# A gated linear attention and mixture-of-experts kernel: every engine's list of operations in a new order

## The reference

```python
h = _ln(x, ln_w, ln_b)
q, k, v = h @ Wq, h @ Wk, h @ Wv
gk = log_sigmoid(h @ gk_w1 @ gk_w2 + gk_b2) / 16
S[t] = exp(gk[t]) * S[t-1] + k[t] * v[t]        # scan over the 256 tokens
o = _rms(q * S, rms_w) * silu(h @ Wg)
x1 = x + o @ Wo
x = _layernorm(x + x1 + gelu(_ln(x1) @ W1 + b1) @ W2 + b2)
scores = softmax(x @ gate_w + gate_b); top 2 of 8
for i in range(8):                               # where expert i is among the two
    out = relu((x * w_i) @ w1[i] + b1[i]) @ w2[i] + b2[i]
x = _layernorm(x + out)
```

## Time and profile before

| what | value |
|---|---|
| median of three runs | 450.14 us (448.68 to 451.42) |
| profiled execution | 452.75 us, of which 451.0 us from the first to the last instruction (the span) |
| mean granted clock of TensorE | 0.965 |
| instructions | 10568 |

### The profile page before, as it was taken

One profiled execution on the slowest core, in us unless ns is written; L12 is line 12 of the kernel. 1 busy time (PEld: TensorE's weight loads), 2 busy tenths in 40 slices (PEclk: granted clock), 3 DMA queues, 4 the chain that ended last, 5 costly groups with the idle time before them and its releaser, 6 DMA issues.

```text
span 451.0 us, 10568 instructions
## 1 busy us (share of the span) xinstructions
PE 405.0 (90%) x2806; PEld 316.7 (70%) x2806; DVE 369.5 (82%) x1216; ACT 344.5 (76%) x980; POOL 326.8 (72%) x299
## 2 busy tenths in 40 slices
PE   5998999899889888999969999788999999999993
PEld 3554555555555555477849768678899999999993
DVE  6379999999999998647875888888777877778874
ACT  2576999999888995998786689467876777777772
POOL 2057799999999997585065556777777887777775
PEclk9999999999999998899996999689999999999997
DMA  7065675765766444070001116356686877776710
GB/s 221 9 164 140 153 175 124 182 155 131 173 141 150 118 121 113 2 233 2 0 25 45 40 41 240 107 149 179 195 261 199 241 204 197 201 208 194 205 59 21
DMA packets 44378, 62.20 MB, mean 138 GB/s; under 512 B 6670, under 2 KB 29713, under 8 KB 42400
## 3 DMA queue, kind: packets, MB, share of 16 engines
q1 hardware_dynamic: 39712, 52.20, 44.9%
q0 software_dynamic: 4320, 8.93, 5.3%
q10 hardware_dynamic: 288, 0.41, 0.3%
HBM read 47.99 MB, written 13.97 MB: 137 GB/s over the span
## 4 chain that ended last, share of the span: by engine, by line
POOL 33%; PE 33%; issue 16%; DVE 10%; ACT 5%; DMA 2%; POOLq 1%; ACTq 0%; DVEq 0%
POOL states L2168 17%; PE bank L761 11%; PE bank L745 10%; POOL o_scale L2180 4%; POOL x_sb L2186 3%; PE bank L395 3%; POOL out_rows L942 3%; POOL row_buffers L2159 3%; POOL slab L2174 2%; PE bank L408 1%; ACT row_buffers L461 1%; PE bank L751 1%; PE bank L384 1%; DVE st L485 1%; PE bank L1129 1%
## 5 line engine op out<-in xcount | busy, mean ns | idle before, releaser
L596 POOL DMA_INDIRECT expert_regions<-row_buffers,row_i x64 | 62.1, 971 | 50.1 <-DVE row_i L580 22.6
L942 POOL DMA_INDIRECT out_rows<-h2t x71 | 70.7, 995 | 30.4 <-issue 24.3
L761 PE MATMUL bank<-ew,h2t 128*128 x568 | 79.1, 283 | 4.6 <-DVE h2t L893 3.2
L2168 POOL TENSOR_TENSOR states<-states,queries 128x1024 f32<-128x1024 f32 x32 | 75.1, 2370 | 7.2 <-DVE states L1906 7.2
L745 PE MATMUL bank<-h2t,slab 128*128 128x128 f32 x568 | 78.4, 282 | 0.5 <-ACT h2t L779 0.5
L761 PEld LDWEIGHTS bank<-ew,h2t 128*128 128x128 f32 x568 | 69.5, 193 | 7.6 <-issue 6.0
L1906 DVE TENSOR_TENSOR_SCAN states<-bank,kv 128x512 f32<-128x512 f32 x64 | 72.9, 1200 | 0.6 <-ACT bank L1443 0.6
L745 PEld LDWEIGHTS bank<-h2t,slab 128*128 128x128 f32 x568 | 70.7, 196 | 1.3 <-issue 0.8
L786 ACT ACTIVATE h2t<-bank,slab 128x128 f32<-128x128 f32 x142 | 43.9, 364 | 9.9 <-PE bank L745 9.9
L884 DVE TENSOR_SCALAR h2t<-bank,slab 128x128 f32<-128x128 f32 x142 | 42.6, 341 | 1.1 <-PE bank L745 0.7
L779 ACT ACTIVATE h2t<-bank 128x128 f32<-128x128 f32 x71 | 19.6, 277 | 26.8 <-PE bank L751 25.2
(11 more groups left out here) (216 smaller groups left out, 925.1 us busy)
## 6 DMA issues: line engine op xcount, KB each, us to landing
slab<-in_slabs SPq DMA_DIRECT2D x71, 258.0 KB
kv<-values_by_head SPq DMA_DIRECT2D x30, 512.0 KB, 6.0
h2t<-expert_regions SPq DMA_DIRECT2D x71, 72.0 KB
x_sb<-in_x SPq DMA_DIRECT2D x32, 128.0 KB, 6.0
values_by_head<-row_buffers SPq DMA_DIRECT2D x15, 256.0 KB, 2.1
out_rows<-h2t POOLq DMA_INDIRECT x71
expert_regions<-row_buffers,row_i POOLq DMA_INDIRECT x64
expert_regions<-pad_record SPq DMA_DIRECT2D x9, 72.0 KB, 3.0
```

The lines of the kernel that those rows point to most:

```text
L596: pool.indirect_dma_start(out=regions, out_offset=bass.IndirectOffsetOnAxis(ap=row_i[:, q, g:g + 1].bitcast(U32), axis=0), in_=rec[:, ring ...
L761: ins = pe.matmul(bank[7][:, 0:D], c_ht[:, s, c * P:(c + 1) * P], ew2[:, bass.ds(e * HC + c * D, D)], start=(c == 0), stop=(c == HC - 1 an ...
L942: pool.indirect_dma_start(out=out, out_offset=bass.IndirectOffsetOnAxis(ap=rc[:, q, D + 1:D + 2].bitcast(U32), axis=0), in_=c_y[:, item % ...
L2168: pool.tensor_tensor(half, half, queries[:, s, :].unsqueeze(1).to_broadcast([P, VL, T]), ALU.mult).then_inc(q_applied, 1)
```

## The change

The four lists of PE, ACT, DVE and POOL are new from the end of the setup to the last slot. The helper functions, their waits, the buffers and SP's list are the same, and each operation is issued as often as before. The loops over pairs and slots are written out, so that pairs and slots can differ in order. The diff has over a thousand lines of calls; these are its parts around the steps spoken of below.

```diff
@@ PE
+            transpose_x(0)
             bias_products()
-            transpose_x(0)
+            project_v(0)
             transpose_x(1)
-            project_v(0)
             project_zq(0)
+            project_v(1)
             project_g(0)
             project_k(0)
             replicate_v(0)
-            project_v(1)
             replicate_v(1)
             replicate_v(2)
             replicate_v(3)
+            transpose_x(2)
+            project_zq(1)
+            project_v(2)
             project_g(1)
             project_k(1)
...
             sum_keys(0, 0)
             sum_keys(0, 1)
-            transpose_x(3)
+            fold_ffn()
             sum_squares(0)
...
-            for k in range(5, PAIRS):
-                sum_keys(k - 3, 0)
-                transpose_second(k - 5)
-                project_k(k - 1)
-                sum_keys(k - 3, 1)
-                transpose_x(k)
-                sum_squares(k - 3)
-                project_v(k)
-                project_zq(k)
-                project_g(k)
-                output_product(k - 3)
...
             sum_squares(13)
+            output_product(12)
             first_product(0)
+            first_product(1)
             output_product(13)
-            first_product(1)
+            first_product(2)
...
+            transpose_rows(0)
             output_product(15)
-            transpose_rows(0)
             second_product(3)
             transpose_rows(1)
             logits(0)
-            first_product(5)
-            second_product(4)
             transpose_rows(2)
             logits(1)
+            second_product(4)
+            first_product(5)
+            logits(2)
...
-            for k in range(27, STEPS_C):
-                expert_step(k)
+            hidden(24)
+            back(23)
+            turn(25)
+            back(24)
+            turn(26)
+            hidden(25)
+            hidden(26)
+            turn(27)
+            back(25)
+            hidden(27)
+            turn(28)
+            back(26)
...
@@ ACT
+            squares(13)
+            sig_exp_of(15)
+            gate_sum(15)
+            sig_log_of(15)
+            z_log_of(15)
+            rstd_heads(13)
+            act.preload_act_table_set("gelu_and_others")
             evacuate_q(15)
-            norm_second(11)
-            z_log_of(15)
-            evacuate_h2t(11)
-            sig_of(14)
-            squares(13)
-            rstd_heads(13)
-            gate_sum(15)
-            act.preload_act_table_set("gelu_and_others")
             gelu(0)
             act.preload_act_table_set("natural_log_exp_and_others")
             decay_of(15)
...
             gelu(3)
+            gelu(4)
+            evacuate(0)
             act.preload_act_table_set("natural_log_exp_and_others")
+            evacuate(1)
+            rstd(0)
             rstd_second(14)
-            evacuate(0)
+            evacuate(2)
             norm_second(14)
+            exps(0)
             act.preload_act_table_set("gelu_and_others")
-            gelu(4)
             gelu(5)
...
@@ DVE
+            copy_projections()
+            stats_first(2)
+            var_first(2)
             scale_rest()
-            stats_first(2)
-            copy_projections()
+            stats_first(3)
+            var_first(3)
             first_keys()
-            var_first(2)
-            stats_first(3)
             outer_piece(0)
+            log_sigmoid(0)
             outer_piece(1)
             outer_piece(2)
-            log_sigmoid(0)
             outer_piece(3)
             scan(0)
-            copy_ffn()
-            var_first(3)
             log_sigmoid(1)
-            stats_first(4)
             outer_product(1)
             scan(1)
+            copy_ffn()
+            stats_first(4)
...
             log_sigmoid(15)
             norm_heads(13)
+            var_second(12)
+            scan(15)
             residual(13)
-            scan(15)
             stats_second(13)
             var_second(13)
             rows_of(0)
+            stats_of(0)
             norm_heads(14)
             rows_of(1)
-            stats_of(0)
+            stats_of(1)
+            split_bias()
+            norm_heads(15)
             residual(14)
...
             choice_of(0, 3)
+            places_of(0)
             logits_of(1)
-            places_of(0)
+            var_second(15)
             choice_of(1, 0)
...
@@ POOL
             norm_first(0)
             norm_first(1)
+            norm_first(2)
+            norm_first(3)
             gate_of(0)
-            norm_first(2)
             apply_q(0, 0)
             apply_q(0, 1)
-            norm_first(3)
             gate_of(1)
+            apply_q(1, 0)
             scale_of_heads(0)
...
+            apply_q(7, 0)
+            apply_q(7, 1)
+            gate_of(8)
+            sum_x(5)
+            scale_of_heads(7)
...
             apply_q(13, 0)
+            scale_of_heads(12)
             apply_q(13, 1)
+            gate_of(14)
+            sum_x(10)
+            apply_q(14, 0)
+            scale_of_heads(13)
             sum_x(11)
-            gate_of(14)
-            scale_of_heads(13)
-            apply_q(14, 0)
             apply_q(14, 1)
+            sum_x(12)
             apply_q(15, 0)
             apply_q(15, 1)
...
             scale_of_heads(15)
-            sum_x(13)
+            scatter(0, 0, 1)
             sum_x(14)
-            scatter(0, 0, 1)
             scatter(0, 1, 2)
             sum_x(15)
...
-            for item in range(21, SLOTS):
-                if BIAS_FROM <= item + 3 < SLOTS:
-                    bias_rows_in(item + 3)
-                store(item)
+            bias_rows_in(30)
+            store(21)
+            store(22)
+            store(23)
+            bias_rows_in(31)
+            store(24)
```

More of the change, by code:

```diff
@@ L1365, in _ @@
+            back(69)
+            back(70)
         @block.scalar
@@ new lines, in _ @@
+            norm_heads(0)
+            scan(2)
+            stats_first(5)
+            residual(0)
+            log_sigmoid(3)
+            var_first(5)
+            stats_second(0)
+            stats_first(6)
+            var_second(0)
+            var_first(6)
+            norm_heads(1)
+            outer_product(3)
+            residual(1)
+            scan(3)
+            stats_second(1)
+            log_sigmoid(4)
+            var_second(1)
+            outer_product(4)
+            norm_heads(2)
@@ new lines, in _ @@
+            scan(4)
+            residual(2)
+            stats_first(7)
+            stats_second(2)
+            log_sigmoid(5)
+            var_second(2)
+            outer_product(5)
+            norm_heads(3)
+            var_first(7)
+            scan(5)
+            residual(3)
+            stats_first(8)
+            stats_second(3)
+            log_sigmoid(6)
+            var_second(3)
+            var_first(8)
+            outer_product(6)
+            norm_heads(4)
+            stats_first(9)
@@ new lines, in _ @@
+            scan(6)
+            residual(4)
+            var_first(9)
+            stats_second(4)
+            log_sigmoid(7)
+            var_second(4)
+            norm_heads(5)
+            outer_product(7)
+            residual(5)
+            stats_first(10)
+            stats_second(5)
+            var_first(10)
+            var_second(5)
+            scan(7)
+            log_sigmoid(8)
+            outer_product(8)
+            norm_heads(6)
+            stats_first(11)
+            scan(8)
@@ new lines, in _ @@
+            residual(6)
+            log_sigmoid(9)
+            stats_second(6)
+            var_first(11)
+            var_second(6)
+            outer_product(9)
+            norm_heads(7)
+            stats_first(12)
+            scan(9)
+            var_first(12)
+            residual(7)
+            log_sigmoid(10)
+            stats_second(7)
+            stats_first(13)
+            var_second(7)
+            norm_heads(8)
+            outer_product(10)
+            var_first(13)
+            residual(8)
@@ new lines, in _ @@
+            scan(10)
+            stats_second(8)
+            log_sigmoid(11)
+            var_second(8)
+            outer_product(11)
+            stats_first(14)
+            norm_heads(9)
+            var_first(14)
+            scan(11)
+            residual(9)
+            log_sigmoid(12)
+            stats_second(9)
+            outer_product(12)
+            var_second(9)
+            norm_heads(10)
+            scan(12)
+            stats_first(15)
+            residual(10)
+            var_first(15)
@@ new lines, in _ @@
+            norm_first(5)
+            gate_of(3)
+            sum_x(0)
+            norm_first(6)
+            apply_q(3, 0)
+            scale_of_heads(2)
+            apply_q(3, 1)
+            gate_of(4)
+            sum_x(1)
+            apply_q(4, 0)
+            scale_of_heads(3)
+            gate_of(5)
+            apply_q(4, 1)
+            norm_first(7)
+            sum_x(2)
+            apply_q(5, 0)
```

(22 more changed lines are left out.)

1377 lines of the change are left out of this document (1097 added, 280 removed).

## The result

| | before | after |
|---|---|---|
| median of 20 runs | 451.19 us (448.19 to 452.92) | 448.00 us (445.42 to 451.39) |
| profiled execution | 452.75 us, span 451.0 | 451.34 us, span 449.5 |

The ratio is 0.9941, 95% interval 0.9922 to 0.9960: faster by 0.6%, some 3 us. The forecast was 436 us, a gain of 14. The sign was right; most of the gain that was forecast isn't there. The 20 executions of after lie up to 6 us apart, the longer ones at a lower mean granted clock (0.970 in the profiled one of 451.34 us, 0.982 to 0.986 in the five shortest), so its trace is that of one of the longest.

A forecast was written before the change was run, and what follows sets the result against it. The prediction took POOL and DVE as saturated in attention's steady part and PE in the experts', no engine bounding the whole. -8.8 - 2.0 - 4.3 + 1.0 = -14.1 gave 436 us by the median; range 429 to 448.

The forecast's parts named there:

- (a): Attention up to the end of `scan(15)`: earlier start, postponed sums and new order of the end gain 8.8 us.
- (b): From `scan(15)` to the first `transpose_rows`: 15.4 us instead of 17.4, with `split_bias` waiting for the experts' loads; gain 2.0.
- (c): Routing up to `turn(0)`: three POOL waits go, against sums among the scatters and a later first scatter; gain 4.3 us.
- (d): Experts: early slots and last scatter keep their slack, steady part nearly the old order; cost 1.0 us.
- two places where `back` follows `back`: Experts' steady part, slots 23/24 and 39/40: each exposes a relu or a row of `z_added`; +1.0 us, bounds 0 and 3.
- the gapless walk: Attention walked: `apply_q(4,0)` at 65.8 us, then POOL without gaps until `apply_q(13,1)` ends at 165.3.
- the 1.5 us for a slow first product: Attention's end: 1.5 us taken off the gain in case `first_product(0)` again runs at the lower clock; bounds 0 and 1.8.
- 2.7 from `sum_x`: Attention's end: ten sums done instead of eleven when `apply_q(13,1)` ends, bringing that point 2.7 us forward.
- the pair's handover: Rival, attention's pairs: POOL waits once per pair for a scan or `o_rs`; 458 us at 2 us a pair; chance 0.08.
- The stall by POOL's sums: Routing: two `sum_x`, four instructions, meet DVE's `choice_of(1)`; 2.0 us added, bounds 0 and 5.1.
- The lead is spent in routing: Rival: attention ends earlier, but routing keeps its pace, with no gain behind `scan(15)`; 442 to 448 us; chance 0.25.
- The change does not do what it says: Rival: start's gaps return as waits inside the pairs, routing stalls move elsewhere; 448 to 452 us; chance 0.07.

The follow-up runs named there:

- Experiment 4: The kernel after the change with only POOL's stores 0 to 10 put back among the scatters as before the change: 445.08 us, ratio 0.9890 to before.
- experiment 9: After with before's stores and the sums of pairs 14 and 15 ahead of the first scatter, plus `sum_x(10)` back ahead of `apply_q(13, 0)`: 442.48 us, ratio 0.9851.
- experiments 7 and 8: After's order to the experts, then before's: 7 moved five POOL operations later, 448.06 us; 8, also with two sums first, moved four ScalarE suppliers earlier, 444.81 us.

## Why the prediction was wrong

The sum in the trace against the forecast's terms, as lengths between the same events:

| term | forecast | trace |
|---|---|---|
| (a) to the end of `scan(15)` (191.18 to 186.38) | -8.8 | -4.8 |
| (b) from there to `transpose_rows(0)` (17.4 to 16.4 us) | -2.0 | -1.0 |
| (c) from there to `turn(0)` (80.0 to 76.25 us) | -4.3 | -3.8 |
| (d) from there to the end of the span (162.4 to 170.5 us) | +1.0 | +8.0 |
| sum | -14.1 | -1.5 |

**(d) failed as a mechanism,** and in the traces it is over half of the miss (7.0 of 12.6 us). The step was: "The last scatter moves with the first, so the records of slot 24 keep their slack." The first scatter did move, the last did not (338.19 us, 337.78 before), since stores that depend on the slots had been put ahead of scatters that don't. I had compared the order of PE's slots, not the order of stores and scatters in POOL's queue. Experiment 4 shows it: with the stores back, the last scatter moves 6.0 us and the time falls by 2 to 3 us. The term also put TensorE's clock in the first slots at nothing. From `turn(0)` to `turn(70)` after's trace takes 158.7 us, that of experiment 4 150.9 and before 151.1; of the 7.7 us between the first two, 4.0 are there at `turn(23)` and are the clock's. So 2 to 3 us of time are shown for the stores; how much the clock costs after in an execution nearer to the median, no trace shows. The other piece of the term, two places where `back` follows `back` for +1.0, had the wrong sign: from `turn(25)` to `turn(70)` after takes 88.2 us, before 89.9.

**(a) was mis-sized,** by 4.0 us, in the gapless walk. `apply_q(4,0)` comes at 67.72 instead of 65.8 (1.9), since DVE's first keys wait for PE to 19.68 instead of 17.3 (18.90 to 20.25 in the other traces with this order). From there to the end of `apply_q(13,1)` at 171.38 it is 103.7 us, not 99.5: POOL's six waits, 3.6 us, where the term allowed 1.0. The attention's end went as walked (15.0 us to the end of the scan, 14.5 in the walk), and the 1.5 us for a slow first product weren't needed: its clock stayed at 1.00. The "2.7 from `sum_x`" is worth 1.8 to 2.6 by experiment 9. Why the ring leaves POOL these waits is open: experiments 7 and 8 tried to remove them from two sides and lengthened the attention by 3.2 and 5.5 us. That is the mechanism of the rival "the pair's handover", at 0.3 us a pair instead of the 1.3 from which it would decide; the two experiments show that it can grow.

**(b) was mis-sized** by 1.0. The wait for the experts' loads came as walked, but `split_bias` took 4.3 us instead of 3.2: its copy took 1.65 us, 0.69 in before, while POOL's scale of the heads ran beside it for 2.14 us instead of 1.27.

```profile
199.34 2.14 POOL L2991 TENSOR_TENSOR o_scale<-slab,o_rs 128x512 f32<-128x512 f32 x1 [3.00 <-ACT o_rs L1723]
```
```profile
200.39 1.65 DVE L825 COPY bias_rows<-kv 128x1024 bf16<-128x1024 bf16 x1
```

**(c) was right in its sum, half right in its parts.** The stall by POOL's sums was priced at 2.0 us, and four instructions lost 4.25 (5.01 less 0.76); removing it gave 3.4 us in time. The first scatter was also later than walked (22.7 us behind `transpose_rows(0)`, not 21.5). Against that, the clock didn't fall in routing (0.98; 0.92 in the earlier trace rows). The Trainium skill, "SBUF — State Buffer", § Who interferes with whom, has the later of the two instructions wait for the whole of the other; by that rule the term was up to 5.1 us, and the trace is much nearer to it than to the 2.0 that I took.

**The rivals.** The 448.00 us stand where two of them meet, by luck. "The lead is spent in routing" (442 to 448) has a mechanism that didn't happen: routing gained 3.8 us. "The change does not do what it says" (448 to 452) had the waits inside the pairs right, and no more. No rival had a store or the clock of the first slots in it.

## What to carry to other kernels

A lead is worth what the last transfer of the next stage makes of it. When an order changes, follow each in-order queue beyond the stage that gains, and ask of each instruction that can wait which independent ones stand behind it: here stores put ahead of scatters cost 2 to 3 us and two sums 3.4, cured by moving the stores behind scatters that don't need the slots and the sums to where the queue idled. Don't price the waits of a saturated ring of engines one by one: moving five waiting operations back, and in another run four of their suppliers forward, cost 4 us each time. And before a stall in one trace is given the whole of a loss, set the same instructions of two traces side by side: half of this one was a clock.

## What the runs showed of the hardware

- Short VectorE instructions with two operands in SBUF took five to ten times as long beside POOL's sums (0.17 us became 1.78, 0.26 became 1.22), each until POOL's instruction ended; and POOL's own instruction was the one that stretched where it began (199.34) behind one of VectorE's that ran to 200.35 (2.14 us instead of 1.27).
- One slot's product took 2.06 us at 1.2 GHz and 1.13 at 2.4. Over three slots in before's order that made 0.4 us of difference, since PE then waited for others; over two slots in after's order, where it waited for nothing, it made 3.7. The clock's price can't be read from the busy time of the slow instructions alone.
